# Two-layer transformer kernel, mixture of experts: tiles of 256 rows replaced by 60 tiles of 256 and 15 of 128

## Time and profile before

| | us |
|---|---|
| three runs | 1517.55, 1521.41, 1516.59; median 1517.55 |
| the profiled execution | 1515.43, its span 1513.5 |
| busy in the span: PE, DVE, ACT, POOL | 1404.1, 1177.3, 817.2, 523.3 |
| expert tiles (first product of tile 0 to last eviction) | 510.8 to 798.2 |
| clock granted to TensorE, mean | 0.984 |

### The profile page before, as it was taken

How to read it: one execution, slowest core, us unless ns; L and a number is a source line. 1 busy time by engine, 2 the same in 40 slices (tenths; PEclk the granted TensorE clock), 3 DMA queues, 4 the chain that set the end, 5 groups by cost and what they waited for, 6 DMA issues and landing times.

```text
span 1513.5 us, 35393 instructions
## 1 busy us (share of the span) xinstructions
PE 1404.1 (93%) x12926; PEld 904.6 (60%) x12926; DVE 1177.3 (78%) x2687; ACT 817.2 (54%) x1562; POOL 523.3 (35%) x942
## 2 busy tenths in 40 slices
PE   5699999999999899999998999999999999999994
PEld 3467677677776799998884444444444444444432
DVE  4789889889888795456677888888888888888752
ACT  2334534544543333334334677777766777776673
POOL 2333234234233111172312244444434444442121
PEclk8999999999999999999999999999999999999997
DMA  4111111111112566776973444333334443332300
GB/s 119 38 42 52 45 48 44 51 47 44 54 33 66 165 208 209 220 245 208 258 195 62 98 106 105 98 98 102 87 93 102 108 103 97 98 92 70 82 9 14
DMA packets 118205, 151.94 MB, mean 100 GB/s; under 512 B 31269, under 2 KB 83109, under 8 KB 113413
## 3 DMA queue, kind: packets, MB, share of 16 engines
q1 hardware_dynamic: 105160, 119.47, 29.0%
q0 software_dynamic: 12880, 30.30, 6.8%
HBM read 108.35 MB, written 40.83 MB: 99 GB/s over the span
## 4 chain that ended last, share of the span: by engine, by line
PE 48%; DVE 32%; POOL 7%; issue 6%; ACT 5%; DMA 1%; SPq 0%; POOLq 0%; DVEq 0%; ACTq 0%
DVE nmax L1516 8%; PE bank L1948 8%; PE bank L1939 8%; DVE P L1205 7%; PE bank L1816 5%; PE bank L1994 5%; PE bank L2017 4%; ACT P L946 3%; PE bank L1773 3%; PE bank L1850 2%; PE bank L1957 2%; PE bank L1864 2%; DVE t L1080 1%; PE bank L2064 1%; DVE t L1078 1%
## 5 line engine op out<-in xcount | busy, mean ns | idle before, releaser
L1516 DVE TENSOR_REDUCE nmax<-bank 128x1 f32<-128x512 f32 (+3 forms) x704 | 428.8, 634 | 84.6 <-PE bank L1994 83.6
L946 ACT ACTIVATE P<-bank 128x512 f32<-128x512 f32 x640 | 371.2, 599 | 183.2 <-PE bank L2017 178.4
L1994 PE MATMUL bank<-KT,QT 76*128 76x512 bf16 (+3 forms) x1024 | 251.3, 303 | 28.5 <-DVE nmax L1516 20.9
L2017 PE MATMUL bank<-QT,KT 78*128 78x512 bf16 (+3 forms) x1024 | 244.5, 301 | 8.9 <-ACT P L946 5.5
L693 POOL DMA_INDIRECT xs_d<-xn,idx x128 | 124.6, 973 | 306.0 <-PE bank L1773 197.9
L1994 PEld LDWEIGHTS bank<-KT,QT 76*128 76x128 bf16 x1024 | 86.8, 97 | 189.1 <-DVE nmax L1516 130.6
L1816 PE MATMUL bank<-P,V 128*32 128x512 f32 (+3 forms) x2048 | 191.3, 447 | 0.0
L1205 DVE TENSOR_TENSOR P<-bank,early_w 128x512 f32<-128x512 f32 x256 | 158.7, 682 | 41.3 <-PE bank L1773 41.2
L910 ACT ACTIVATE hr<-bank 128x512 f32<-128x512 f32 x142 | 84.8, 597 | 175.0 <-PE bank L1939 172.1
L741 POOL DMA_INDIRECT hT<-ys_d,idx x104 | 103.5, 995 | 159.9 <-PE bank L2017 141.8
L2017 PEld LDWEIGHTS bank<-QT,KT 78*128 78x128 bf16 x1024 | 98.6, 98 | 85.0 <-ACT P L946 31.9
(11 more groups left out here) (257 smaller groups left out, 2228.6 us busy)
## 6 DMA issues: line engine op xcount, KB each, us to landing
QT<-parts_d SPq DMA_DIRECT2D x96, 192.0 KB
P<-in_fc SPq DMA_DIRECT2D x71, 256.0 KB, 2.9
P<-in_proj SPq DMA_DIRECT2D x71, 256.0 KB, 3.2
parts_d<-parts SPq DMA_DIRECT2D x32, 384.0 KB, 2.5
P<-xs_d SPq DMA_DIRECT2D x71, 128.0 KB, 3.0
ys_d<-P POOLq DMA_DIRECT2D x71, 128.0 KB, 3.4
KT<-parts_d SPq DMA_DIRECT2D x64, 128.0 KB
KT<-parts_d SPq DMA_DIRECT2D x32, 192.0 KB
```

What stands on the lines that cost most here:

```text
L946: nc.scalar.activation(P[s % 2][:, u, :], bank[k % 2][:, :], ACT.Exp, scale=float(DH) ** -0.5).then_inc(s_sb, 1)
L1516: nc.vector.tensor_reduce(nmax[:, s // TWO, h:h + TWO * nh - 1:TWO, j], max_bank(n, k)[:, 0:nh * w].rearrange("p (h w) -> p h w", h=nh), A ...
L1994: ins = pe.matmul(max_bank(n, k)[:, i * w:(i + 1) * w], QT[n.p][0:MROWS, h, j * 128:(j + 1) * 128], KT[n.p][0:MROWS, h, 0:w], start=True, ...
L2017: ins = pe.matmul(bank[k % 2][:, c:c + n], KT[b.p][0:SROWS, h, 128 * kb:128 * kb + 128], QT[b.p][0:SROWS, h, 128 * kb:T], start=True, stop ...
```

## The change

An expert's last piece is now a half tile where it fits: HT = 128 rows. 60 tiles of 256 rows (FULL) and 15 of 128 (HALF) are the most that 16384 rows can need in this cut; 75 tiles in a fixed order, SEQUENCE, in which half tiles stand at index 19, 22, 25, 28, 31, 34, 37, 42, 46, 50, 54, 58, 62, 66 and 70. Every step of a tile takes `z = tile_rows(t)` rows. The plan gets new steps for the half tiles (k = 9 to 11), a fourth round of the conversion and a last placing step; it ends at k = 19 instead of 14. All 75 tiles are written out. The constants of the second layer's start move: FIRST's gathers at 40 to 43, SECOND's at 44 to 47, combine at 45 and 50, third gathers at 62 to 69 and their combine at 71, MAX0 = 61. In the diff below context lines are left out, `nc.vector.` is not written and indentation is cut.

```diff
-NTILES = (2 * CAP + E * (GT - 1)) // GT
-SPARE = NTILES - 2 * CAP // GT
+HT = GT // 2
+FULL = (2 * CAP // HT - E) // 2
+HALF = (2 * CAP + E * (HT - 1)) // HT - 2 * FULL
+SOON = E - 1
+SEQUENCE = []
+for _k in range(FULL):
+  SEQUENCE.append(_k)
+  if 18 <= _k <= 30 and _k % 2 == 0:
+    SEQUENCE.append(FULL + (_k - 18) // 2)
+  if 34 <= _k <= 55 and _k % 3 == 1:
+    SEQUENCE.append(FULL + SOON + (_k - 34) // 3)
+NTILES = len(SEQUENCE)
...
+SPARE = E - 1
+def tile_rows(t):
+  return GT if SEQUENCE[t.known()] < FULL else HT
...
-LOOPED = 8
-STRAIGHT = 4
-GATHER0, COMBINE0, MAX0, GATHER2, COMBINE2 = 33, 41, 57, 52, 63
+ROUTES_TILE = 32
+AFTER_AHEAD = tuple(SEQUENCE.index(E * a - 1) + 1 for a in AHEAD_TILES[1:])
+GATHER0, COMBINE0, MAX0, GATHER2, COMBINE2 = 40, 45, 61, 62, 71
-for t in range(STRAIGHT * TB):
-  body(Turn(t // TB, t % TB, TB))
-with eng.Fori(STRAIGHT, LOOPED) as i:
-  for p in range(TB):
-    body(Turn(i, p, TB))
-for t in range(LOOPED * TB, NTILES):
+for t in range(NTILES):
...
+z = tile_rows(t)
...
+if k + 1 == SEQUENCE.index(FULL):
+  sp.wait_ge(plan_ready, 5)
-if k == LOOPED * TB:
+if k == ROUTES_TILE:
-if k == LOOPED * TB + 1:
+if k == ROUTES_TILE + 1:
...
+z, r0 = tile_rows(t), ys_row(t)
+pool.dma_start(ys_d[r0:r0 + z, :].rearrange("(c p) d -> p c d", p=128), yg[t.p][:, 0:z // 128, :]).then_inc(ys_stored[t.p], 16)
...
-pool.wait_ge(ys_stored[p], 16 * (E * AHEAD_TILES[1] // TB))
+pool.wait_ge(ys_stored[p], 16 * len(range(p, AFTER_AHEAD[0], TB)))
-pool.wait_ge(ys_stored[p], 16 * (E * AHEAD_TILES[2] // TB))
+pool.wait_ge(ys_stored[p], 16 * len(range(p, AFTER_AHEAD[1], TB)))
...
-nc.scalar.copy(xgT[t.p % 2], bank[0][:, 0:GT]).then_inc(xgT_sb, 1)
+z = tile_rows(t)
+nc.scalar.copy(xgT[t.p % 2][:, 0:z], bank[0][:, 0:z]).then_inc(xgT_sb, 1)
-  nc.scalar.activation(hr[k][:, :], bank[2 + 2 * (t.p % 2) + k][:, :], ACT.Relu).then_inc(e_relu, 1)
+  nc.scalar.activation(hr[k][:, 0:2 * z], bank[2 + 2 * (t.p % 2) + k][:, 0:2 * z], ACT.Relu).then_inc(e_relu, 1)
...
-  plan(tensor_tensor(cnt, fill[:, :], ebase[:, 0, :], ALU.subtract))
+  plan(scalar_tensor_tensor(out=cnt, in0=fill[:, :], scalar=float(-HT), in1=ebase[:, 0, :], op0=ALU.add, op1=ALU.subtract))
...
-    plan(tensor_reduce(tabf[:, k, :], sums(k), AX.X, ALU.add))
+    plan(tensor_reduce(tabf[:, k, 0:FULL], sums(k), AX.X, ALU.add))
...
+def half_counts():
+  plan(tensor_tensor(cnt, fill[:, :], ebase[:, 0, :], ALU.subtract))
+  plan(tensor_tensor(cmp, cnt.unsqueeze(2).to_broadcast([128, E, CAP // GT]),
+                 steps[:, :].unsqueeze(1).to_broadcast([128, E, CAP // GT]), ALU.is_gt))
+  plan(tensor_reduce(odd, cmp, AX.X, ALU.add))
+  plan(tensor_tensor(odd, odd, nt, ALU.subtract))
+  plan(tensor_scalar(used, starts[2], -1.0, float(FULL), ALU.mult, ALU.add))
+  plan(tensor_scalar(used, used, 0.0, None, ALU.max))
+  plan(tensor_tensor(used, used, nts[2], ALU.min))
+  plan(tensor_tensor(used, used, nt, ALU.add))
+  plan(tensor_tensor(used, used, nts[2], ALU.subtract))
+  plan(tensor_tensor(left, nt, used, ALU.subtract))
+  plan(scalar_tensor_tensor(out=left, in0=left, scalar=2.0, in1=odd, op0=ALU.mult, op1=ALU.add))
+def running(into, of):
+  plan(tensor_tensor(cum, incl[:, :, :], of.unsqueeze(1).to_broadcast([128, E, E]), ALU.mult))
+  plan(tensor_reduce(into, cum, AX.X, ALU.add))
+def half_bounds():
+  plan(tensor_scalar(few, nt, float(AHEAD_TILES[2]) - 0.5, None, ALU.is_lt))
+  plan(tensor_tensor(odd, left, few, ALU.mult))
+  plan(tensor_tensor(tmp, left, odd, ALU.subtract))
+  running(from_, odd)
+  running(last_, tmp)
+  plan(tensor_scalar(last_, last_, from_[:, E - 1:E], None, ALU.add))
+  plan(tensor_tensor(from_, from_, odd, ALU.subtract))
+  plan(tensor_tensor(last_, last_, tmp, ALU.subtract))
+  plan(tensor_tensor(from_, from_, last_, ALU.subtract))
+  plan(tensor_tensor(from_, from_, few, ALU.mult))
+  plan(tensor_tensor(from_, from_, last_, ALU.add))
+  plan(tensor_tensor(last_, from_, left, ALU.add))
+def half_tiles():
+  numbers = tiles[:, 0, 0:HALF].unsqueeze(1).to_broadcast(narrow)
+  plan(tensor_tensor(half_in, numbers, from_.unsqueeze(2).to_broadcast(narrow), ALU.is_ge))
+  plan(tensor_tensor(half_row, numbers, last_.unsqueeze(2).to_broadcast(narrow), ALU.is_lt))
+  plan(tensor_tensor(half_in, half_in, half_row, ALU.mult))
+  plan(scalar_tensor_tensor(out=base_d, in0=used, scalar=float(GT), in1=ebase[:, 0, :], op0=ALU.mult, op1=ALU.add))
+  plan(scalar_tensor_tensor(out=tmp, in0=from_, scalar=float(-HT), in1=base_d, op0=ALU.mult, op1=ALU.add))
+  plan(scalar_tensor_tensor(out=terms, in0=tiles[:, 0, 0:HALF], scalar=float(-HT), in1=tiles[:, 1, 0:HALF], op0=ALU.mult, op1=ALU.add))
+  plan(tensor_tensor(half_row, terms.unsqueeze(1).to_broadcast(narrow),
+                 tmp.unsqueeze(2).to_broadcast(narrow), ALU.add))
+  plan(tensor_tensor(half_row, half_row, half_in, ALU.mult))
+  plan(tensor_tensor(half_exp, half_in, ebase[:, 1, :].unsqueeze(2).to_broadcast(narrow), ALU.mult))
+  for k, part in enumerate((half_row, half_exp)):
+    plan(tensor_reduce(tabf[:, k, FULL:], part.rearrange("p e t -> p t e"), AX.X, ALU.add))
+  plan(tensor_tensor(tab[:, FULL:NTILES], tabf[:, 0, FULL:], tiles[:, 2, 0:HALF], ALU.add))
+  tensor_copy(tab[:, NTILES + FULL:2 * NTILES], tabf[:, 1, FULL:]).then_inc(plan_ready, 1)
-  plan(tensor_scalar(step_a, starts[0], float(GT), None, ALU.mult))
-  plan(tensor_tensor(step_a[:, 1:E], starts[0][:, 1:E], starts[2][:, 0:E - 1], ALU.subtract))
-  plan(tensor_scalar(step_a[:, 1:E], step_a[:, 1:E], float(GT), later[2] - float(REGION), ALU.mult, ALU.add))
-  plan(tensor_scalar(base_b, ebase[:, 0, :], later[1], None, ALU.add))
-  plan(tensor_scalar(base_c, ebase[:, 0, :], later[2], None, ALU.add))
+  plan(tensor_tensor(tmp, starts[2], used, ALU.add))
+  plan(tensor_scalar(tmp, tmp, float(GT), float(HALF * HT) - later[2], ALU.mult, ALU.add))
+  plan(scalar_tensor_tensor(out=step_d, in0=from_, scalar=float(HT), in1=tmp, op0=ALU.mult, op1=ALU.subtract))
+  plan(tensor_scalar(step_a, starts[0], float(GT), float(HALF * HT), ALU.mult, ALU.add))
+  plan(scalar_tensor_tensor(out=tmp, in0=used, scalar=2.0, in1=from_, op0=ALU.mult, op1=ALU.subtract))
+  plan(tensor_scalar(tmp, tmp, float(HT), float(-REGION), ALU.mult, ALU.add))
+  plan(tensor_tensor(step_a[:, 1:E], step_a[:, 1:E], tmp[:, 0:E - 1], ALU.add))
+  for base, h in ((base_b, 1), (base_c, 2)):
+    plan(tensor_scalar(base, ebase[:, 0, :], later[h], None, ALU.add))
+    plan(tensor_tensor(base, base, base_d, ALU.min))
-  if h < 2:
-    plan(tensor_tensor(slot_all2, slot_all2 if h else slot_all, moved[:, :], ALU.add))
-  else:
-    tensor_tensor(idx_all[:, :], slot_all2, moved[:, :], ALU.add).then_inc(rows_ready, 1)
+  plan(tensor_tensor(slot_all2, slot_all2 if h else slot_all, moved[:, :], ALU.add))
+def rows_placed():
+  plan(tensor_scalar(moved[:, :], slot_all2, float(SOON * HT), float(FULL * GT), ALU.is_ge, ALU.mult))
+  plan(tensor_scalar(slot_all, slot_all2, float(HALF * HT), float((SOON - HALF) * HT - FULL * GT), ALU.is_ge, ALU.mult))
+  plan(tensor_tensor(slot_all, slot_all, slot_all2, ALU.add))
+  tensor_tensor(idx_all[:, :], slot_all, moved[:, :], ALU.add).then_inc(rows_ready, 1)
-  other_tiles(ahead, NTILES)
+  other_tiles(ahead, FULL)
+  half_counts()
+if k == 10:
+  half_bounds()
+if k == 11:
+  half_tiles()
+if k == 12:
-if k == 10:
+if k == 13:
-if k == 11:
+if k == 14:
-if k == 12:
+if k == 15:
-if k == 13:
+if k == 16:
-if k == 14:
+if k == 17:
-if k == 15:
+  rows_above(base_d)
+if k == 18:
+  rows_moved(step_d)
+  rows_summed(3)
+if k == 19:
+  rows_placed()
+if k == 20:
...
-  h = hr[k][:, :].rearrange("p (k t) -> p k t", k=2)
-  tensor_tensor(hT[:, t.p % 2, 2 * k:2 * k + 2, :], h, h, ALU.mult).then_inc(e_sq, 1)
+  z = tile_rows(t)
+  h = hr[k][:, 0:2 * z].rearrange("p (k t) -> p k t", k=2)
+  tensor_tensor(hT[:, t.p % 2, 2 * k:2 * k + 2, 0:z], h, h, ALU.mult).then_inc(e_sq, 1)
...
-    ins = pe.matmul(w[:, i * GT:(i + 1) * GT], wfc[t.p][:, c * 128:(c + 1) * 128], xgT[t.p % 2], start=True, stop=True)
+    z = tile_rows(t)
+    ins = pe.matmul(w[:, i * z:(i + 1) * z], wfc[t.p][:, c * 128:(c + 1) * 128], xgT[t.p % 2][:, 0:z], start=True, stop=True)
-for c in range(GT // 128):
+for c in range(tile_rows(t) // 128):
```

More of the change, by code:

```diff
@@ L40, with ys_row @@
 TB = 4
-NTILES = (2 * CAP + E * (GT - 1)) // GT
-SPARE = NTILES - 2 * CAP // GT
+HT = GT // 2
[10 more added lines that the diff above has]
+NTILES = len(SEQUENCE)
+assert NTILES == FULL + HALF and sorted(SEQUENCE) == list(range(NTILES))
+SPARE = E - 1
 DUMMY = E * REGION
 NROWS = DUMMY + SPARE * GT
+def tile_rows(t):
+    return GT if SEQUENCE[t.known()] < FULL else HT
+def ys_row(t):
+    n = SEQUENCE[t.known()]
+    if n < FULL:
+        return SOON * HT + n * GT
+    return (n - FULL) * HT + (FULL * GT if n - FULL >= SOON else 0)
 LN_EPS = 1e-5
@@ L739, in gather @@
                     ahead = E * AHEAD_TILES[1 if n.less(L2 + 2) else 2]
-                    rows = ys_d[0:ahead * GT, :] if n.less(L2 + 3) else ys_d[:, :]
```

(27 more changed lines are left out.)

67 lines of the change are left out of this document (49 added, 18 removed).

## The result

The changed kernel took 1523.68 us in the median (1516.70 to 1530.34, 19 runs) against 1516.23 us (1513.25 to 1521.73, 19 runs) for the kernel before on the same chip: ratio 1.0045, 95% interval [1.0032, 1.0057]. By the ratio it is slower by about 6.8 us (the medians differ by 7.5). The forecast was 1518 within 1509 to 1526, with no change as the likeliest verdict. The time lies in the range, but by the forecast's own line of 0.3% the kernel is slower, which it had given 0.26, and the slowdown is larger than forecast.

What follows compares the result with a forecast made beforehand. PE was taken to bound plain expert tiles at 3.73 us each. Terms -12.7 + 2.2 + 5.3 + 5.0 + 1.8 = +1.6 us on 1515.43 gave 1517.0, forecast as 1518 after half the run-median offset; range 1509 to 1526.

Steps and rivals of the forecast that it cites:

- Term 1: Expert tiles on PE: 71 full tiles become 60 full and 15 half, -12.7 us, all in the last 30 tiles.
- weight-load rival: First product of half tiles on PE: 192 ns weight loads set the pace, +19 us, about 1537; chance 0.02.
- Term 2: Behind a half tile PE waits for ACT's row copy, 0.28 us at each of 8 half tiles: +2.2 us.
- Term 3: Planning steps from k=9 on exceed DVE's room per tile, so PE waits: +5.3 us.
- Term 4: Near index 45 to 49, gathers closer to their combine make DVE wait for rows and root: +5.0 us on PE.
- Term 5: DMA queueing in the last tiles +1.0, SP's wait at index 33 +0.3, combine at 71 +0.5: +1.8 us.
- late-weights rival: Weights land too late, so half tiles 50 to 66 save nothing: +9.2 us, about 1527; chance 0.22.
- rival "faster": PE's bound rules while DVE and POOL are covered: -6.5 us, about 1510; chance 0.28.

Runs made afterwards that it cites:

- run 9: Changed kernel with planning spread over tiles 9 to 28 and COMBINE0 = 46, MAX0 = 62: 11.4 us off the changed kernel, ratio 0.9970 to the kernel before.
- run 2: Changed kernel with ACT's copy of the next tile's rows between the two relus: 1524.03 us, ratio 1.0044 to the kernel before.
- run 1: Changed kernel with the same plan steps spread over tiles 9 to 28: 1515.76 us, ratio 1.0009 to the kernel before.
- run 11: Changed kernel with spread planning, combining from tile 46 and the row copy between the relus: by the ratios 5 us worse than run 9.
- run 3: Changed kernel with SP's six route and residual row transfers spread over tiles 33 to 37: 1522.08 us, ratio 1.0056 to the kernel before.
- run 10: Run 9 plus last gathers two a tile from tile 61, combine at 67: last step 4.49 us (5.83 in run 9), tile 68 to 69 7.36 instead of 4.86.
- run 5: Changed kernel with COMBINE0 = 46 and MAX0 = 62, one tile later: 1529.05 us, ratio 1.0003 to the kernel before.

## Why the forecast was right in kind and short in size

Its terms beside what the traces and runs give:

```
                                       forecast   measured
1 rows of work                          -12.7     pitch 0.11 as used: -12.7
2 handover, 8 half tiles                 +2.2     8 x 0.40 = +3.2
3 planning on DVE                        +5.3     +6.8, less 1.8 before: +5.0
4 combine and root                       +5.0     +5.4
5 SP block                               +0.3     +2.3
5 queueing and the end                   +1.5     +4.3
not told apart, mostly behind tile 45             +1.0
sum                                      +1.6     +8.5, by the copies
```

Terms 4 and 5 (the end) are measured against run 9, the others against the plain pattern.

- **Term 1** held where nothing else makes PE wait: records of 128 columns stand 0.11 us apart. So the weight-load rival is out, in which a load of 192 ns sets the pace. The Trainium skill (TensorE: Matmul & The Clock Gate, Back-to-back issue gap) gives such pairs about 81 ns at 128 columns and 131 ns at 512, so fewer columns save less than in proportion; the trace of the changed kernel does not agree, with 0.89 us for eight records of 128 columns against 1.73 for eight of 256.
- **Term 2** named the right place and wait, and run 2 shows it. Its size missed 0.12 per half tile. The gap itself is 0.31; the forecast's own numbers give 2.43 + 0.37 + 0.14 - 2.62 = 0.32, which it had rounded to 0.28. The rest is in the transpose and first product behind the gap, which the forecast took as unchanged.
- **Term 3** was right in mechanism, and run 1 shows it by taking it away. Its size was close too. The forecast's 5.3 is net of what the plan cost before, and that was 1.8 us: steps of 4.34, 4.38, 3.92 and 4.05 instead of 3.73 at tiles 7, 11, 15 and 16. In the changed kernel it cost 6.8: the 6.5 that run 1 took away and 0.3 that run 1 still has at tile 11. Net that is 5.0.
- **Term 4** was right in mechanism, and in size partly by luck: tiles 47 to 51 took 18.8 us against 13.4 in run 9, where the combine has its rows. PE's 2.15 us are what was worked out, from a landing that was 1.3 later and a POOL that was 1.0 sooner than taken. Of the other 3.2 us the half clock, which was in no term, is 1.7, so the root is left with about 1.6 instead of 3.1.
- **Term 5 is the step that failed.** "The wait of SP for rows_stored at index 33 now stands between half tiles (+0.3)" counted SP's wait and not that half tiles shorten the time between the issue and the use of the weights behind the six transfers, from 4.7 us to 3.2; that cost 2.3. At the end, "combine at 71 on +0.5" took the wait and not what is queued behind it: compared with run 9, the last step costs 2.6 more (1.5 of it at half clock) and tile 67 to 68 1.7 more. Behind tile 45 the landing of the second weight piece sets the end in places, as the late-weights rival has it; DMA share at 735 to 770 rose to 0.89 from 0.83, yet with a quarter of the half tiles' weights only some 2 us came back.

That the time lies in the range owes something to its width: the stage lost 8.5 us where 1.6 were forecast.

The rival "faster" was wrong in size, not in its condition: with planning and combine covered (run 9) the kernel is faster, at 0.9970 of before, about 1512 on the forecast's scale, where it said 1510. So here 15 half tiles were worth their work only when nothing bunched stood beside them. The kernel before was not run with the same two edits, and its own plan cost it 1.8 us, so how much of run 9's 0.3% is due to the half tiles is not shown. What also stays open is why the early copy makes run 11 slower than run 9 behind tile 45, beyond that stalls of PE appear at other tiles, and how much of any single saving at tiles 57 to 70 comes back: there the steps take 3 to 8 us, and which transfer falls on which tile may decide them.

## What to carry to other kernels

When a change makes some steps of a pipeline shorter, recount what each other engine does per step, not in total: the plan's work was unchanged in run 1 and 5.5 us came from its spacing, and one tile's shift of the combine gave 6.4. For a moved wait, count all that its engine issues behind it, and how long before its use each of these must land. Judge single fixes together as well: an early copy that removed its own stall won nothing, twice (runs 2 and 11).

## What the runs showed of the hardware

The granted clock fell to half for 3.4 us after short stalls of PE, and a stall of 2 us then cost 3 to 4: 8 records of 256 columns took 3.64 us instead of 1.89. Such stretches began behind idle gaps of 2.15 and 2.59 us in the changed kernel, 2.04 in run 2, 2.52 in run 3, 1.37 in run 10 and 1.05 in run 5. But the length of the gap alone didn't decide: a gap of 3.06 us at 791.2 in run 3, one of 2.45 at 720.9 in run 9 and one of 1.86 at 730.8 in the kernel before brought none. In counting a stall here, the half clock belongs to its price as a chance of some 1.7 us (1.7 at 684.3 and 1.5 at 790.1 in the changed kernel).

Weights of 256 KB landed 3.5 us after their issue in the median of the changed kernel's expert stage (second piece), but 6.8 us after it among other transfers at a DMA share of 0.99 (run 2).
